# Fetching the first self-attention stacks in three places, reordering DVE's finish and maxima, and storing the last rows tile by tile

## The chip, the cores and the metric

The kernel runs on one core of one Trainium2 chip. The metric is the device time of one execution in microseconds. Engines are named as in the profile: PE multiplies matrices, DVE and ACT are the vector and the scalar engine, POOL is the general one, SP issues nearly all DMAs.

## What is computed

Two transformer layers over x of 8 batches of 512 rows and 512 columns, in float32. The first is a cross-attention on a context of 77 rows with adaptive layer norm. The second is a block with self-attention, cross-attention and an MLP. The parts that matter here, from the reference:

```
x_norm = modulate(_ln(x), shift_a, scale_a)
qkv = x_norm @ W_qkv + b_qkv
...
attn_w = softmax(einsum('bhqd,bhkd->bhqk', q, k) * scale)     # 16 heads of 32
attn_out = einsum('bhqk,bhkd->bhqd', attn_w, v) ... @ W_proj + b_proj
x = x + gate_a[:, None] * attn_out
...
h = gelu(modulate(_ln(x), shift_m, scale_m) @ W_mlp1 + b_mlp1) @ W_mlp2 + b_mlp2
x = x + gate_m[:, None] * h
```

## The kernel before

Six stages follow each other over all 8 batches: preparation, the first cross-attention, qkv, self-attention, the second cross-attention, the MLP. Each stage keeps its result in device memory for the next. A matrix product is made of three products of high and low parts, so 12 matmuls of 128x512 make one 128x512 block of a product over 512 rows. Work is split in tiles of 128 rows (NT = 4 of a batch) and in groups of four heads (G = 4 of a batch, 32 groups in all).

The order of every engine is written by hand: one program (`run` of each stage) is walked once per engine, and each step emits what that engine does for it, or nothing. `braid` takes one step of each of its generators in turn; such a turn is called a round here. `weave` and `next(following)` pull steps of the next stage into this one. An engine executes its list in order, so what stands behind a wait waits too.

**qkv** (class `Qkv`). For each batch b it makes eight products of queries and keys, m = 0 to 7, and four of values. PE writes a product into one of three banks, ACT adds the bias and writes the high part into one of three slots of `out_parts` (L1590), DVE the low part (L1531), SP stores both (L1512). ACT may overwrite a slot when its store has landed; PE may overwrite a bank when DVE has read it. Between the products the norm of batch b + 1 is made (`turning`): SP loads 1 MB into `norm_x` right behind the first store of the batch (L302), DVE takes statistics (L312) between the low parts of m = 3 and m = 4, normalises (L321) around that of m = 6, and PE turns the rows from the end of m = 7 on (L354). In the batches 6 and 7 the first maxima of self-attention are woven in.

**The first stacks.** Self-attention's group n needs a query stack and a key stack in local memory. `fetch(n)` issues six DMAs of 256 KB on SP (L1731, L1734), and on DVE, for n under 4, a fill of two rows with ones (L1801). In `SelfAttention.run`, fetch(0), fetch(1), fetch(2) and load_values(0) make up one step; `Qkv.run` pulls it at the end of batch 4. Whatever SP issues later, the next store and the load of `norm_x` too, is behind them.

**Self-attention** (class `SelfAttention`). A group n has 16 rounds. In each PE makes one block of scores (L1899), on which ACT takes an exponential (L1977), and one block of scores of group n + 2 (L1878), whose row maxima DVE takes (L1813, the maxima). There are two banks for scores, so PE's score i waits for exponential i - 2, and three for the maxima. `finish(n - 1)` closes the group before: ACT copies its heads out (L1990, round 2); DVE turns the sums (L1827, round 10), inverts them (L1830), spreads them (L1833), multiplies (L1839, round 13); ACT takes the high part of the result (L1999, between the exponentials of rounds 14 and 15), DVE the low part (L1844, round 15). POOL adds pairs of exponentials, 128x2048 in one operation (L1779), twice a group. PE's sums (L1933) and value products (L1921) come in bursts. `max_rows` turns the maxima of group n + 1 in round 2. In the second to fourth group of a batch PE has the projection of the batch before between the scores: from round 4 on in the second group, from round 0 in the third (six matmuls a round) and the fourth (three).

The braid of a group before:

```
yield from braid(s.attend(n), s.maxima(n + self.MAX) ..., after(2, s.max_rows(...)) ..., s.finish(n - 1) ..., *side)
```

**MLP** (class `Mlp`). Per batch 16 hidden blocks j. PE's down products of block j go into four accumulators, one per tile, three matmuls each (L2177); they trail the up products by two blocks. After the last up product (j = 15) come the down products of 13, 14 and 15. Then `residual`: DVE multiplies each accumulator by the gate (L2144), adds it to `x_rows` (L2146), and SP stores the batch, 1 MB, when all four are done (L2111).

## Time and profile before

| what | value |
|---|---|
| times of three runs | 2584.04, 2582.30, 2569.95 us; median 2582.3 |
| the profiled execution, its own time | 2574.66 us |
| its span | 2572.9 us |
| granted PE clock, mean | 0.972 of full |
| busy, share of the span | PE 93%, DVE 54%, ACT 40%, POOL 23% |
| DMA | 354 MB, 138 GB/s in the mean |

The span is what the rows below cut up; 1.8 us lie around it. The matmuls' ends are modelled, so PE's share says more of how densely they were issued than of spare time. The stages by time in the span: qkv from about 500 to 825 us, self-attention from 825 to 1475, the MLP from about 1856 to the end. Times of the rows count from the start of the span.

### The profile page before, as it was taken

To read this page: it belongs to the slowest core of one execution; us is meant where nothing else is said; L and a number is where in the kernel's file an instruction comes from. 1 tells how busy PE (TensorE), PEld (TensorE's weight loads), DVE (VectorE), ACT (ScalarE), POOL (GpSimd) and SP (SyncE) were. 2 spreads that over 40 slices of the span, in tenths; PEclk is the share of its full clock that TensorE was granted. 3 is DMA by queue.
4 is the path that set the end of the run, shared out by engine and by line. 5 is a ranking of instruction groups with operands and counts; after the bars stand their busy time and mean duration, and the time that the engine had idled before them with its cause. 6 is when DMAs were issued, how large, how long until landed. Compare 5 with 4: busy or idle time off the path is not lost. (4 is left out here: it accounts for less than half of the span.)

```text
span 2572.9 us, 32327 instructions
## 1 busy us (share of the span) xinstructions
PE 2401.8 (93%) x12048; PEld 1683.8 (65%) x12048; DVE 1380.0 (54%) x2463; ACT 1026.1 (40%) x1831; POOL 588.1 (23%) x325
## 2 busy tenths in 40 slices
PE   6889999999979899999998789999899999999998
PEld 5656666678867344444444456766588888888887
DVE  4566666644546877776777456676743222222221
ACT  3454444423322455555554334444442322233231
POOL 2101111110000466665665411111211011101100
PEclk9899999999989899999999899999999999999999
DMA  6687777554564446565453568786531101110110
GB/s 205 193 216 229 206 216 200 173 197 176 180 212 147 104 112 153 132 153 130 116 144 90 146 157 221 200 230 184 166 114 58 58 1 58 58 58 1 58 42 17
DMA packets 261275, 354.19 MB, mean 138 GB/s; under 512 B 60979, under 2 KB 109195, under 8 KB 261118
## 3 DMA queue, kind: packets, MB, share of 16 engines
q1 hardware_dynamic: 259950, 348.27, 47.9%
q0 software_dynamic: 1168, 3.85, 0.4%
q8 instruction: 96, 1.57, 0.3%
q14 instruction: 61, 0.50, 0.1%
HBM read 233.78 MB, written 116.69 MB: 136 GB/s over the span
## 5 line engine op out<-in xcount | busy, mean ns | idle before, releaser
L1813 DVE TENSOR_REDUCE negated_max<-banks 128x1 f32<-128x512 f32 x512 | 331.8, 675 | 140.7 <-PE banks L1878 140.4
L1977 ACT ACTIVATE self_exponentials<-banks 128x512 f32<-128x512 f32 x512 | 286.3, 594 | 283.8 <-PE banks L1899 133.0
L1779 POOL TENSOR_TENSOR self_exponentials<-self_exponentials,self_exponentials 128x2048 f32<-128x2048 f32 x64 | 303.1, 4736 | 217.0 <-ACT self_exponentials L1977 217.0
L2177 PE MATMUL banks<-mlp_w_down_hi,out_parts 128*128 128x512 f32 x1024 | 333.8, 389 | 0.1
L337 POOL TENSOR_SCALAR norm_rstd<-norm_mean_var 128x4 f32<-128x4 f32 x32 | 8.0, 249 | 1336.3 <-DVE norm_mean_var L316 1336.3
L2134 DVE TENSOR_TENSOR out_parts<-wide,out_parts 128x512 fp32r<-128x512 f32 x128 | 93.1, 727 | 371.6 <-ACT out_parts L2206 371.6
L1899 PE MATMUL banks<-self_query_stack,self_key_stack 98*128 98x512 f32 x512 | 236.4, 463 | 26.3 <-ACT self_exponentials L1977 23.5
L2196 ACT ACTIVATE wide<-banks,bias_columns 128x512 f32<-128x512 f32 x128 | 88.3, 690 | 426.0 <-PE banks L396 425.9
L1899 PEld LDWEIGHTS banks<-self_query_stack,self_key_stack 98*128 98x128 f32 x512 | 98.1, 192 | 212.6 <-ACT self_exponentials L1977 173.3
L2177 PEld LDWEIGHTS banks<-mlp_w_down_hi,out_parts 128*128 128x128 f32 x1024 | 192.2, 188 | 40.4 <-DVE cross_last_x_rows L1261 0.5
L1878 PE MATMUL banks<-self_key_stack,self_query_stack 96*128 96x512 f32 x512 | 207.4, 408 | 2.3 <-DVE negated_max L1813 2.1
L2177 PE MATMUL banks<-mlp_w_down_lo,out_parts 128*128 128x512 f32 x512 | 199.2, 389 | 0.0
L1217 DVE TENSOR_REDUCE negated_max<-banks 128x4 f32<-128x308 f32 x256 | 121.0, 473 | 100.4 <-PE banks L396 96.7
L1921 PE MATMUL banks<-self_exponentials,self_values 128*32 128x512 f32 x1024 | 140.4, 621 | 0.7 <-ACT self_exponentials L1977 0.7
L312 DVE BATCH_NORM_STATS2 norm_stats<-norm_x 128x6 f32<-128x512 f32 x128 | 84.6, 671 | 67.0 <-DMA norm_x<-x 66.7
L1400 ACT ACTIVATE cross_exponentials<-banks 77x512 f32<-77x512 f32 x128 | 75.3, 591 | 106.6 <-PE banks L1318 106.6
L377 ACT ACTIVATE wide<-banks,modulation_columns 128x512 f32<-128x512 f32 x96 | 74.5, 776 | 104.7 <-PE banks L354 97.3
L396 PE MATMUL banks<-x_hi,w_qkv_hi 128*128 128x512 f32 x256 | 101.2, 395 | 16.0 <-DVE out_parts L1531 15.1
L1590 ACT ACTIVATE out_parts<-banks,bias_columns 128x512 fp32r<-128x512 f32 x64 | 44.1, 689 | 179.6 <-PE banks L396 144.1
L1400 ACT ACTIVATE L_exponentials<-banks 77x512 f32<-77x512 f32 x128 | 75.3, 591 | 87.9 <-PE banks L1318 87.7
L2177 PEld LDWEIGHTS banks<-mlp_w_down_lo,out_parts 128*128 128x128 f32 x512 | 96.1, 188 | 20.0
L1878 PEld LDWEIGHTS banks<-self_key_stack,self_query_stack 96*128 96x128 f32 x512 | 99.8, 195 | 14.2 <-DVE negated_max L1813 5.6
(208 smaller groups left out, 5253.4 us busy)
## 6 DMA issues: line engine op xcount, KB each, us to landing
L_query_stack<-q_parts_L SPq DMA_DIRECT2D x96, 256.0 KB, 4.8
norm_x<-x SPq DMA_DIRECT2D x24, 1024.0 KB, 7.5
self_query_stack<-q_parts_self SPq DMA_DIRECT2D x96, 256.0 KB, 4.0
self_key_stack<-k_parts_self SPq DMA_DIRECT2D x96, 256.0 KB, 6.3
cross_query_stack<-q_parts_cross SPq DMA_DIRECT2D x96, 256.0 KB, 5.0
x_rows<-x SPq DMA_DIRECT2D x23, 1024.0 KB, 6.7
x<-x_rows SPq DMA_DIRECT2D x22, 1024.0 KB, 5.0
q_parts_L<-out_parts SPq DMA_DIRECT2D x32, 512.0 KB, 4.6
```

The source lines that it names most:

```text
L396: mm = e.matmul(out_ap, l, r, start=i == 0, stop=i == len(terms) - 1)
L1217: e.tensor_reduce(k.nm[n % 2][:, t:GH * NT:NT], k.bank[:, bk, 0:GH * S].rearrange("p (h k) -> p h k", k=S), AX_X, ALU.max, negate=True).th ...
L1400: e.activation(self.p[:, i % self.HEADS_KEPT, :], k.bank[0:S, self.scores.of["score", i], :], ACT.Exp, scale=SCALE).then_inc(self.exp.sem, 1)
L1779: e.tensor_tensor(self.p[kt - 1][:], self.p[kt - 1][:], self.p[kt][:], ALU.add).then_inc(self.paired.sem, 1)
L1813: e.tensor_reduce(k.nm[n % 2][:, h * NT + t:h * NT + t + 1], k.bank[:, self.max_banks.of["max", i], :], AX_X, ALU.max, negate=True).then_i ...
L1878: e.matmul(k.bank[:, bk, :], self.q[n % 4][0:ST, h, t * P:(t + 1) * P], self.keys[n % 4][0:ST, h, :], start=True, stop=True).then_inc(self ...
L1899: e.matmul(k.bank[:, bk, :], self.keys[n % 4][0:ST_MAX, h, kt * P:(kt + 1) * P], self.q[n % 4][0:ST_MAX, h, :], start=True, stop=True).the ...
L1921: mm = e.matmul(k.bank[h * HD:(h + 1) * HD, bk, :], self.v[n % 3][:, kt, h * HD:(h + 1) * HD], self.p[kt][:, h, :], start=kt == 0, stop=kt ...
L1977: e.activation(self.p[kt][:, h, :], k.bank[:, self.scores.of["score", i], :], ACT.Exp, scale=SCALE).then_inc(self.exp.sem, 1)
L2134: e.tensor_tensor(h[:, 1, :], k.wides[k.wide_turns.of["up", i]][:], raw(h[:, 0, :]), ALU.subtract).then_inc(self.lo.sem, 1)
L2177: mm = e.matmul(bank, l, w, start=j == 0 and q == 0, stop=j == JC - 1 and q == 2)
L2196: e.activation(k.wides[w][:], k.bank[:, self.banks.of["up", i], :], ACT.Gelu_apprx_tanh, bias=k.bias_cols[:, col:col + 1]).then_inc(self.w ...
```

## The change

1. `SelfAttention.run` now makes three steps of the first fetches: fetch(0); fetch(1); fetch(2) with load_values(0). `Qkv.run` pulls the first at the end of batch 4, the second in batch 5 after the product m = 4, the third at the end of batch 5.
2. In the braid of a self-attention group `finish(n - 1)` stands ahead of `maxima` and `max_rows`.
3. In the last batch of the MLP the down products of j = 14 and 15 run tile by tile, and the rows are stored in four DMAs of 256 KB, each behind its tile's addition.

```diff
@@ Qkv.run @@
                 if b >= B - 2:
                     weave(some(b - B + 3, following))
+                elif b == B - 3 and m == G:
+                    next(following)
                 yield
...
             weave(turning)
-            if b == B - 4:
+            if B - 5 < b < B - 2:
                 next(following)
@@ SelfAttention.run @@
         for n in range(self.FETCH):
             s.fetch(n)
-        s.load_values(0)
-        yield
+            if n == self.FETCH - 1:
+                s.load_values(0)
+            yield
...
-            yield from braid(s.attend(n), s.maxima(n + self.MAX) if n + self.MAX < LAST else None,
-                             after(2, s.max_rows(n + self.ROWS)) if n + self.ROWS < LAST else None,
-                             s.finish(n - 1) if n else None, *side)
+            yield from braid(s.attend(n), s.finish(n - 1) if n else None, s.maxima(n + self.MAX) if n + self.MAX < LAST else None,
+                             after(2, s.max_rows(n + self.ROWS)) if n + self.ROWS < LAST else None, *side)
@@ Mlp.run @@
-            for j in range(JC - self.LAG + 1, JC):
-                s.down(b, j)
+            rest = range(JC - self.LAG + 1, JC)
+            if b < B - 1:
+                for j in rest:
+                    s.down(b, j)
+            else:
+                for t in range(NT):
+                    for j in rest:
+                        s.down(b, j, (t,))
             s.residual(b)
@@ Mlp.sync @@
         def residual(b):
+            if b == B - 1:
+                for t in range(NT):
+                    sp.wait_ge(*self.added(b * NT + t))
+                    e.dma_start(k.out[b, t * P:(t + 1) * P, :], k.x[:, t, :]).then_inc(self.last_stored.sem, 16)
+                return
```

DVE's wait in `residual` follows the new count of down steps in the last batch (`last_step`), and the last batch's stores have a semaphore of their own.

SP from the last value stores of qkv's batch 4 on, before:

```order
L1517 DMA v_self<-qkv_value_rows_145 128x512
L1731 DMA self_query_stack_148<-q_parts_self 32x4x512 x3
L1734 DMA self_key_stack_152<-k_parts_self 32x4x512 x3
L1731 DMA self_query_stack_149<-q_parts_self 32x4x512 x3
L1734 DMA self_key_stack_153<-k_parts_self 32x4x512 x3
L1731 DMA self_query_stack_150<-q_parts_self 32x4x512 x3
L1734 DMA self_key_stack_154<-k_parts_self 32x4x512 x3
L1708 DMA self_values_162<-v_self 128x4x128
L1512 DMA q_parts_self<-out_parts_66 128x2x512
L302 DMA norm_x<-x 128x4x512
```

and with the change:

```order
L1519 DMA v_self<-qkv_value_rows_145 128x512
L1733 DMA self_query_stack_148<-q_parts_self 32x4x512 x3
L1736 DMA self_key_stack_152<-k_parts_self 32x4x512 x3
L1514 DMA q_parts_self<-out_parts_66 128x2x512
L302 DMA norm_x<-x 128x4x512
L1514 DMA q_parts_self<-out_parts_64 128x2x512
L1514 DMA q_parts_self<-out_parts_65 128x2x512
L1514 DMA q_parts_self<-out_parts_66 128x2x512
L1514 DMA k_parts_self<-out_parts_64 128x2x512
L1733 DMA self_query_stack_149<-q_parts_self 32x4x512 x3
L1736 DMA self_key_stack_153<-k_parts_self 32x4x512 x3
```

Six stack DMAs instead of eighteen stand ahead of batch 5's first store and its norm load. The third six, with the values, stand in the same way ahead of batch 6's first store and norm load. DVE's three fills move with them.

DVE in rounds 9 to 15 of a group, before:

```order
L1827 STREAM_TRANSPOSE sums_turned<-banks 128x512
L1813 TENSOR_REDUCE negated_max_83<-banks 128x1
L1830 RECIPROCAL reciprocals_turned<-sums_turned 128x16
L1813 TENSOR_REDUCE negated_max_83<-banks 128x1
L1833 STREAM_TRANSPOSE sums_turned<-reciprocals_turned 128x512
L1813 TENSOR_REDUCE negated_max_83<-banks 128x1
L1839 TENSOR_TENSOR heads_float_1_79<-heads_float_1_79,sums_turned 128x512
L1813 TENSOR_REDUCE negated_max_83<-banks 128x1 x2
L1844 TENSOR_TENSOR heads_parts_73<-heads_float_1_79,heads_parts_73 128x512
L1813 TENSOR_REDUCE negated_max_84<-banks 128x1 x3
```

and with the change, where one maximum fewer stands ahead of the first row:

```order
L1829 STREAM_TRANSPOSE sums_turned<-banks 128x512
L1815 TENSOR_REDUCE negated_max_83<-banks 128x1
L1832 RECIPROCAL reciprocals_turned<-sums_turned 128x16
L1815 TENSOR_REDUCE negated_max_83<-banks 128x1
L1835 STREAM_TRANSPOSE sums_turned<-reciprocals_turned 128x512
L1815 TENSOR_REDUCE negated_max_83<-banks 128x1
L1841 TENSOR_TENSOR heads_float_1_79<-heads_float_1_79,sums_turned 128x512
L1815 TENSOR_REDUCE negated_max_83<-banks 128x1 x2
L1846 TENSOR_TENSOR heads_parts_73<-heads_float_1_79,heads_parts_73 128x512
L1815 TENSOR_REDUCE negated_max_83<-banks 128x1
L1815 TENSOR_REDUCE negated_max_84<-banks 128x1 x3
```

The whole chain is one maximum further ahead, and the maximum of round 15 comes behind the low part. On ACT the copy of the heads (L1990) and the high part of the turned maxima (L1962) change places in round 2.

## Rows read from the trace of the kernel before

**Rows 1.** Timeline, ACT, qkv: start, duration, line, operation, [idle before, releaser].

```profile
665.02 0.69 ACT L1590 ACTIVATE out_parts<-banks,bias_columns 128x512 fp32r<-128x512 f32 x1 [4.06 <-PE banks L396]
...
699.62 0.69 ACT L1590 ACTIVATE out_parts<-banks,bias_columns 128x512 fp32r<-128x512 f32 x1 [4.06 <-PE banks L396]
...
752.38 0.69 ACT L1590 ACTIVATE out_parts<-banks,bias_columns 128x512 fp32r<-128x512 f32 x1 [4.06 <-PE banks L396]
```

**Rows 2.** Timeline, PE, the same stage.

```profile
683.86 0.60 PE L354 MATMUL banks<-identity,norm_x 128*128 128x128 f32 x4
...
728.59 0.80 PE L396 MATMUL banks<-x_hi,w_qkv_hi 128*128 128x512 f32 x1 [15.14 <-DVE out_parts L1531]
```

**Rows 3.** Timeline, SP (its DMA issues), same place.

```profile
698.04 1.65 SPq L1731 DMA_DIRECT2D self_query_stack<-q_parts_self  x3
```

**Rows 4.** Windows, PE and DMA: stretch, length, busy us by engine, granted clock, DMA share, GB/s.

```profile
698.00:721.00 23.00, 15.45 (x67) 12.14 (x66) 7.46 (x6) 2.07 (x3) 0.00 (x0) 0.91 1.01 219
721.00:727.00 6.00, 0.00 (x0) 0.00 (x0) 0.40 (x1) 0.69 (x1) 0.00 (x0) 0.50 1.07 376
```

**Rows 5.** Timeline, DVE, same place.

```profile
675.43 1.29 DVE L312 BATCH_NORM_STATS2 norm_stats<-norm_x 128x6 f32<-128x512 f32 x2 [3.49 <-DMA norm_x<-x]
...
682.73 0.99 DVE L321 TENSOR_SCALAR norm_x<-norm_x,norm_mean_var,norm_rstd 128x512 f32<-128x512 f32 x2
...
698.07 1.76 DVE L1801 MEMSET self_key_stack<- 2x2048 f32 x1 [0.48 <-issue]
...
726.60 1.28 DVE L312 BATCH_NORM_STATS2 norm_stats<-norm_x 128x6 f32<-128x512 f32 x2 [20.07 <-DMA norm_x<-x]
```

**Rows 6.** Waits, 832 to 1440 us: engine, line, releaser: us, times, longest.

```profile
ACT heads_parts L1999 <- DVE heads_float L1839: 23.7, 30, 1.6
PE banks L1899 <- ACT self_exponentials L1977: 23.5, 31, 1.9
```

**Rows 7.** Timeline, ACT and PE, a group's last rounds.

```profile
983.51 0.62 ACT L1999 CAST heads_parts<-heads_float 128x512 fp32r<-128x512 f32 x1 [0.73 <-DVE heads_float L1839]
...
984.68 0.50 PE L1899 MATMUL banks<-self_query_stack,self_key_stack 98*128 98x512 f32 x1 [1.04 <-ACT self_exponentials L1977]
```

**Rows 8.** Timeline, PE, into a group with projection work.

```profile
1041.35 0.50 PE L1899 MATMUL banks<-self_query_stack,self_key_stack 98*128 98x512 f32 x1 [0.34 <-ACT self_exponentials L1977]
```

**Rows 9.** Timeline, DVE, the same group as rows 7.

```profile
979.10 0.69 DVE L1813 TENSOR_REDUCE negated_max<-banks 128x1 f32<-128x512 f32 x1 [1.71 <-PE banks L1878]
979.71 0.70 DVE L1827 STREAM_TRANSPOSE sums_turned<-banks 128x512 f32<-128x512 f32 x1
...
984.60 0.68 DVE L1844 TENSOR_TENSOR heads_parts<-heads_float,heads_parts 128x512 fp32r<-128x512 f32 x1
```

**Rows 10.** Timeline, POOL's addition, DVE's slow subtraction, PE's wait.

```profile
984.71 4.99 POOL L1779 TENSOR_TENSOR self_exponentials<-self_exponentials,self_exponentials 128x2048 f32<-128x2048 f32 x1 [4.29 <-ACT self_exponentials L1977]
...
864.55 4.99 DVE L266 TENSOR_TENSOR self_w_p_lo<-weight_stage,self_w_p_hi 128x512 fp32r<-128x512 f32 x1
...
870.20 0.29 PE L1887 MATMUL banks<-identity,negated_max 128*16 128x128 f32 x1 [2.94 <-DVE negated_max L1813]
```

**Rows 11.** Timeline, the end, DVE, PE and SP.

```profile
2557.83 0.69 DVE L2134 TENSOR_TENSOR out_parts<-wide,out_parts 128x512 fp32r<-128x512 f32 x1 [4.75 <-ACT out_parts L2206]
...
2566.57 0.68 DVE L2144 TENSOR_TENSOR wide<-banks,mlp_gate_and_bias 128x512 f32<-128x512 f32 x1
...
2559.20 0.39 PE L2177 MATMUL banks<-mlp_w_down_lo,out_parts 128*128 128x512 f32 x1
...
2563.97 0.39 PE L2177 MATMUL banks<-mlp_w_down_lo,out_parts 128*128 128x512 f32 x1
...
2568.00 0.39 SPq L2111 DMA_DIRECT2D out<-x_rows  x1
```

**Rows 12.** Lines L2111 and L1517 of SP: issue to landing, us.

```profile
DMA to landing us min/median/max: 4.3/4.3/4.3
...
DMA to landing us min/median/max: 2.0/2.0/2.6
```

More of the change, by code:

```diff
@@ L2024, in __init__ @@
         c = k.count
-        self.x_loaded, self.x_stored = c("dma_x_rows", B, 16), c("dma_x_out", B, 16)
+        self.x_loaded, self.x_stored = c("dma_x_rows", B, 16), c("dma_x_out", B - 1, 16)
+        self.last_stored = c("dma_last_rows_out", NT, 16)
         self.gate_loaded = c("dma_mlp_gate", B, 32)
@@ L2058, in hidden_slot, with last_step @@
         return (2 * G * (B - 1) + i) % 3
+    def last_step(self, b, t):
+        return (b * JC + JC - 1) * NT + t if b < B - 1 else (b + 1) * JC * NT - 1 - (NT - 1 - t) * (self.LAG - 1)
     def set_freed(self, parts, x, gt, wides, third_out):
@@ L2138, in residual @@
                 i = b * NT + t
-                dve.wait_ge(*self.down((b * JC + JC - 1) * NT + t))
+                dve.wait_ge(*self.down(self.last_step(b, t)))
                 dve.wait_ge(*self.gate_loaded(b))
@@ L2161, in up, with down @@
                           self.norm.chunk(pe, b))).then_inc(self.up.sem, 1)
-        def down(b, j):
+        def down(b, j, tiles=range(NT)):
             i = b * JC + j
@@ L2168, in down @@
             pe.wait_ge(*self.w.ready(self.down_at[j]))
-            for t in range(NT):
+            for t in tiles:
                 if j == 0:
```

## Prediction

> **What bounds the kernel now.** I read the page first: PE is busy for 93% of the span, no other engine for more than 54%, so time is lost where PE stands still, and the change acts at three such places. I took each with the timeline of its stretch, then the waits by line.
>
> *In qkv* the first product of a batch is a ruler [rows 1]: batch 4 begins at 665.02, batch 5 at 699.62, batch 6 at 752.38. A batch takes 34.60 us, and batch 5 takes 52.76: **18.2 us too many**. The same turn shows on PE [rows 2]: in batch 4 it turns the normalised rows from 683.86 on, without a pause; in batch 5 it has waited 15.14 us at 728.59. SP is the reason: at 698.04 it issues the first of 18 stack fetches in a row [rows 3]. Each is 256 KB, 4.7 MB in all; at the 219 GB/s of the following 23 us [rows 4] they take 21.5 us, with every DMA engine busy. Behind them come the store and the 1 MB of `norm_x`, in a stretch at 376 GB/s in which PE does nothing and its granted clock is 0.50, the lower of its two levels, 1.2 GHz [rows 4]. DVE gets the rows at 726.60 after 20.07 us of waiting; in batch 4 it got them at 675.43 after 3.49 [rows 5].
>
> *In self-attention* the waits by line give ACT 23.7 us in 30 waits of the high part (L1999) for DVE's product (L1839), and PE 23.5 us in 31 waits of a score for an exponential [rows 6]. They are one chain: ACT takes the high part 0.73 us late, exponential 15 stands behind it, and PE's second score of the next group at 984.68 has waited 1.04 us [rows 7]. Into a fourth group, where projection matmuls lie between the scores, PE waits 0.34 [rows 8]; into a third, with six of them, I found no wait.
>
> *At the end* DVE and one last store stand behind PE's last matmul, and nothing runs beside them.
>
> **A, the fetches.** No DMA goes away. Ahead of batch 5's norm load stand six fetches instead of eighteen: 1.57 MB at 219 GB/s, 7.2 us; then the store, 512 KB, and 1 MB of rows: 1.57 MB again, at the 376 GB/s that such loads reached [rows 4] 4.2 us. Of the 28.56 us between 698.04 and 726.60 the before has 2.9 left when 21.5 and 4.2 are taken off; for the start of the burst I take 1.9 of these, since some is its drain. That is 13.3 us, near 711.3, or 11.7 us behind batch 5's first product. In batch 4 the rows came 10.4 us behind it (675.43 less 665.02), DVE's last normalised pair ended at 683.72 and PE took them at 683.86 [rows 2, 5]. So there is no slack, and what comes later than in batch 4 counts fully: 1.3 us. The fill of the second fetch (1.76 us, L1801) [rows 5] now lies in DVE's norm work in the middle of batch 5; less the part of a wait that it fills, 1.1. Batch 5 costs 2.4. The twelve DMAs' issuing and traffic in mid-batch have cover: the next norm load is a batch away, and each slot of `out_parts` is needed only two products after its store. Batch 6's boundary is as batch 5's, with 256 KB of values more (1.2 us at 219 GB/s) and DVE with maxima to take: 3. Gain 18.2 - 5.4 = **12.8 us**. Bounds: 18.2 if both late loads are absorbed, 6 if each boundary loses a third of what one lost.
>
> **B, the finish ahead of the maxima.** In rounds 9 to 15 DVE's list is the same but for one maximum, which comes last. At 979.10 DVE has waited 1.71 us for a block and only then turns the sums (0.70, L1827) [rows 9]. Now the turn fills that gap, and a maximum (0.69, some 0.6 in sequence) leaves the chain: the product is 1.2 to 1.3 us sooner. ACT's mean wait is 23.7 / 30 = 0.79, and 1.6 at the longest [rows 6]: nearly all of it goes, and next in line is PE's own rate. The gain is what PE felt. It has 16 places of the first kind [rows 7], 16 x 0.79 = 12.6, six of the second [rows 8], 6 x 0.34 = 2.0, and eight without. Sum **14.7 us** of the 23.5. Zero is the lower bound, if another wait follows; 18 the upper, with some of the other waits on exponentials. The maximum put last belongs to a group two ahead, with three banks behind it, and ACT's exchange in round 2 moves a copy past row maxima that are not needed before the next group: nothing. L1844 must begin before POOL's addition, which starts when exponential 15 ends: 984.60 against 984.71 [rows 9, 10], 0.11 us. That becomes about 0.5, since the product comes sooner by more than exponential 15 does.
>
> **C, the end.** PE takes 0.68 us for a tile's three matmuls: from 2559.20, block 14, to 2563.97, the last tile of block 15 [rows 11], seven such steps. Tile by tile, a tile is done every 1.36 us, and DVE's pair takes 1.33 (2 x 0.68). So DVE begins the last pair behind PE's last matmul, at 2564.65 instead of 2566.57: 1.9 us. Low part 15 is ready at 2558.52 (2557.83 and 0.69), and PE now wants it at 2559.88, 1.4 us later: hidden. The stores: SP issued 1 MB at 2568.00 and it landed 4.3 us later [rows 11, 12]; 256 KB of qkv's values land after 2.0 [rows 12]. That saves 2.3, and three earlier quarters go during DVE's pairs. **4.2 us.** Bounds: 1.9, if the landing does not shrink, and 4.9. Here a page speaks against the change. The row shows 2.0 us for one 256 KB transfer. The Trainium skill, "DMA: Bandwidth & Descriptors", section "Rules for kernel authors", wants 1 MiB per DMA for full bandwidth and small transfers put together. Should the four queue one behind another, see the fourth rival.
>
> The sum is 12.8 + 14.7 + 4.2 = **31.7 us**. From the profiled execution's 2574.66 that gives 2543; it was 7.6 us below the median of the three runs, 2582.3, and the mean of all four is 2577.7, which gives 2546. I say **2545**.
>
> **The rivals.** *One: the fetches still hold the norm.* The boundaries are now two, and the first burst's 7.2 us were costed at nearly nothing because other loads have their place behind it. If each costs 8 us or more (SP waits, the rate of 219 GB/s holding for the norm too, 7.2 us instead of 4.2, and PE's return at the low clock), A gives about 1, the sum is 20 and the time 2557. For it: no slack [rows 2]. Against: two thirds of the bytes have gone from the spot. *Two: B's time goes into the next wait.* ACT is one step from PE in every round, and DVE's maxima come later. Then only A and C count, 17: 2561. For it: ACT waits in many places; against: in rows 7 PE waits longer than ACT. *Three, the slower side: L1844 loses its place to POOL.* POOL's addition of 4.99 us begins at the end of exponential 15, and where DVE's subtraction (L266, the same form) met it, it took 4.99 us instead of 0.68, and PE waited 2.94 for a maximum [rows 10]. The chain now ends ACT's part sooner as well; if exponential 15 gained more than L1844 did, by over 0.5 us, the subtraction would fall into every addition: 30 groups x 2.94 = 88 lost, 17 gained, 2648. Against: both start from the same product, and L1844 has one step less before it. This stretch has a page, too: the Trainium skill, "GPSIMD Engine Reference", section 1, says POOL shares its interfaces to local memory with DVE, and names DVE instructions with two inputs there; the trace agrees, 4.99 against 0.68. *Four: small stores queue.* The first quarter is issued at 2559.20 + 1.36 + 1.33 = 2561.9. If they go one after another and each takes the 4.3 us of the only store to the output that a row shows [rows 12], the last lands at 2579.1 instead of 2572.3: C costs 6.8 instead of giving 4.2, and the time is 2556. Against: at 2.0 us each [rows 12] they would be through at 2569.9 even so. *Five: the order moves but no wait does* (DVE's gap [rows 9] is then the block's and not the turn's, and the rows load late for a reason other than the fetches): C alone, about 2573.
>
> **How the numbers follow.** Forecast 0.63; rivals one 0.13, two 0.12, three 0.03, four 0.04, five 0.05. The sum at its upper bounds is 41 us (18.2, 18, 4.9); A at its lower bound with B half met (7) and C at 1.9 makes 15: 2537 to 2563, and the runs shown lie up to 8 us from that mean. The range, 2531 to 2562, takes in rivals one, two and four. This kernel's measurement can tell 0.5%, 13 us, from no change: faster means below 2565. Forecast, rivals one, two and four lie there, with some 0.07 of them, where two terms fail together, on the wrong side: faster 0.85; same 0.10, slower 0.05.
>
> **What would show it.** Batch 5 of qkv takes 37 us and batch 6 no more than 3 over its old length; DVE's L312 waits about 5 us and not 20; PE has no idle of 15. ACT's wait for the product (L1839 before) falls from 23.7 to under 5 us, PE's for exponentials from 23.5 to about 9, and the subtraction of L1844 keeps its 0.68. The last store is issued near the end less 2.0 us, and the one before it 1.3 sooner. Wrong would be: an idle stretch of over 5 us at a batch boundary, PE's scores waiting for the same sum under another releaser, or subtractions of 2 to 5 us on DVE.

## The result and the profile after

| what | before | after |
|---|---|---|
| median | 2578.7 us (2569.95 to 2584.04, four runs) | 2551.9 us (2542.04 to 2553.79, four runs) |
| ratio, 95% interval | | 0.9888 [0.9856, 0.9921] |
| span of the profiled execution | 2572.9 | 2550.1 |
| busy, share of the span | PE 93%, DVE 54% | PE 94%, DVE 55% |

The change makes the kernel 1.1% faster, 29 us by the ratio. A second measurement on another chip, below, gives 0.9858. The forecast was 2545, with a range of 2531 to 2562. In the changed kernel the lines from qkv on stand two further down, those of the MLP's last stores and products 15 to 18.

The first products of the batches 5, 6 and 7 of qkv, timeline of ACT, after; [rows 1] has the same line before:

```profile
710.10 0.69 ACT L1592 ACTIVATE out_parts<-banks,bias_columns 128x512 fp32r<-128x512 f32 x1 [4.06 <-PE banks L396]
...
746.90 0.69 ACT L1592 ACTIVATE out_parts<-banks,bias_columns 128x512 fp32r<-128x512 f32 x1 [4.06 <-PE banks L396]
...
786.63 0.69 ACT L1592 ACTIVATE out_parts<-banks,bias_columns 128x512 fp32r<-128x512 f32 x1 [4.51 <-PE banks L396]
```

Batch 5 takes 36.80 us instead of 52.76. Batch 6 takes 39.73; before it took 37.44. Both together give 13.7 us. The norm of batch 6, timeline of DVE in batch 5, answers to [rows 5], and PE's first turn to [rows 2]:

```profile
721.47 1.29 DVE L312 BATCH_NORM_STATS2 norm_stats<-norm_x 128x6 f32<-128x512 f32 x2 [4.45 <-DMA norm_x<-x]
...
726.02 1.76 DVE L1803 MEMSET self_key_stack<- 2x2048 f32 x1 [0.48 <-issue]
...
730.05 0.99 DVE L321 TENSOR_SCALAR norm_x<-norm_x,norm_mean_var,norm_rstd 128x512 f32<-128x512 f32 x2
```

```profile
731.11 0.66 PE L354 MATMUL banks<-identity,norm_x 128*128 128x128 f32 x4 [1.93 <-DVE norm_x L321]
```

The rows reach DVE 11.37 us behind the batch's first product, and the forecast was 11.7; the 10.4 of batch 4 before [rows 1, 5] are missed by 1.0. Then the second stack's fill of 1.76 us stands in DVE's list, ahead of the normalising; DVE's last normalised pair begins 19.95 us behind the first product instead of 17.71, and PE waits 1.93 us. That is batch 5's 2.2 us.

Self-attention, waits by line (engine, line, releaser: us, times, longest), after, the stretch as long as in [rows 6]:

```profile
PE banks L1880 <- DVE negated_max L1815: 5.1, 3, 4.6
...
PE banks L1901 <- ACT self_exponentials L1979: 4.9, 18, 0.8
...
ACT heads_parts L2001 <- DVE heads_float L1841: 1.1, 2, 0.9
```

ACT's wait for the product is gone but for two, and PE's for exponentials goes from 23.5 to 4.9 us. A wait of 4.6 us for a maximum, at one place, is longer than what stood there before. The subtraction of [rows 9] has more room in front of POOL's addition, 0.46 us where it had 0.11, timelines of DVE and POOL:

```profile
973.21 0.68 DVE L1846 TENSOR_TENSOR heads_parts<-heads_float,heads_parts 128x512 fp32r<-128x512 f32 x1
```

```profile
973.67 4.65 POOL L1781 TENSOR_TENSOR self_exponentials<-self_exponentials,self_exponentials 128x2048 f32<-128x2048 f32 x1 [3.45 <-ACT self_exponentials L1979]
```

Once a batch it takes 1.80 us, beside POOL's additions for the projection (L1764); before it took 1.79 there, so the change has no part in that.

The end, timelines of DVE and SP and the landing of the last stores, answers to [rows 11, 12]:

```profile
2539.33 0.69 DVE L2152 TENSOR_TENSOR out_parts<-wide,out_parts 128x512 fp32r<-128x512 f32 x1 [4.75 <-ACT out_parts L2224]
...
2546.11 0.69 DVE L2162 TENSOR_TENSOR wide<-banks,mlp_gate_and_bias 128x512 f32<-128x512 f32 x1
```

```profile
2543.48 4.41 SPq L2126 DMA_DIRECT2D out<-x_rows  x4
```

```profile
DMA to landing us min/median/max: 2.0/2.0/2.0
```

The last pair begins 6.8 us behind the start of the last low part (8.7 before), and each of the four quarters lands 2.0 us after its issue. From the start of that low part to the end of the span it is 10.8 us, and it was 15.0.

These stretches say 13.7, 17.1 and 4.3 us, 35 in all, but the spans differ by 22.8. The gap lies ahead of the change, where both programs are the same: the first product of qkv comes at 509.47 before and 520.78 after. In the windows view of that stretch, before and after, the number behind the five engines' busy times is PE's granted clock:

```profile
150.00:450.00 300.00, 284.05 (x1710) 197.23 (x1709) 194.15 (x407) 142.42 (x261) 40.98 (x36) 0.97 0.79 217
```

```profile
150.00:450.00 300.00, 283.98 (x1665) 198.19 (x1664) 188.74 (x397) 139.26 (x255) 37.99 (x34) 0.94 0.78 213
```

0.94 instead of 0.97 over 300 us of the first cross-attention. Of the twelve kernels below ten began qkv between 507.5 and 512 us; two began at 516.0 and 519.2, with 0.96 and 0.94 there. An execution differs by some 10 us for this, whatever the kernel. So below a part is read from its own stretch, and the timed ratio is its check.

### The profile page after: what moved, and what is told of

Read it like the earlier page. It is cut to its first block, busy times and chain, and to the rows that moved or that the text cites. A ratio compares the mean times of both kernels' runs of the same rounds, so it can differ in the third digit from the quotient of the medians.

```text
span 2550.1 us, 32330 instructions
## 1 busy us (share of the span) xinstructions
PE 2408.3 (94%) x12048; PEld 1688.5 (66%) x12048; DVE 1390.8 (55%) x2463; ACT 1025.2 (40%) x1831; POOL 582.4 (23%) x325
## 4 chain that ended last, share of the span: by engine, by line
PE 81%; DVE 7%; ACT 4%; issue 3%; DMA 3%; SPq 1%; POOL 1%; DVEq 0%; ACTq 0%; POOLq 0%
PE banks L396 43%; PE banks L2195 14%; PE banks L1901 6%; PE banks L1923 4%; PE banks L1880 4%; PE banks L1935 2%; PE banks L1318 2%; PE banks L1332 2%; PE banks L1339 2%; PE banks L354 2%; DMA norm_x<-x 1%; ACT wide L377 1%; DVE negated_max L1815 1%; DVE norm_x L321 1%; PE banks L765 1%
## 5 line engine op out<-in xcount | busy, mean ns | idle before, releaser
L1781 POOL TENSOR_TENSOR self_exponentials<-self_exponentials,self_exponentials 128x2048 f32<-128x2048 f32 x64 | 294.5, 4602 | 202.5 <-ACT self_exponentials L1979 202.5
L329 DVE TENSOR_TENSOR x_lo<-wide,x_hi 128x512 fp32r<-128x512 f32 x80 | 56.3, 704 | 94.0 <-ACT x_hi L379 93.8
```

What stands on the lines that cost most here:

```text
L1781: e.tensor_tensor(self.p[kt - 1][:], self.p[kt - 1][:], self.p[kt][:], ALU.add).then_inc(self.paired.sem, 1)
```

## The experiments

The table has all of them. Batch 5 and 6 are the distances of their first products in qkv. *Stage* reaches from ACT's last product of queries and keys in qkv to its last high part of heads in self-attention; *first three* and *last batch* are the distances between the high parts of groups 0 and 3, and of groups 27 and 31. *End* reaches from the start of the MLP's last low part to the end of the span. All us, from one profiled execution each; the median and the ratio are of timed runs against the kernel before on the same chip. The rounds in these names count from 1, those of the text on the kernel before from 0: round 8 is `after(7, ...)`. (The expectation of the first try counts from 0.)

| kernel | median | ratio, 95% | batch 5 | batch 6 | stage | first three | last batch | end |
|---|---|---|---|---|---|---|---|---|
| before | 2578.7 | | 52.8 | 37.4 | 664.2 | 62.8 | 100.1 | 15.0 |
| the change | 2551.9 | 0.9888 [0.9856, 0.9921] | 36.8 | 39.7 | 647.1 | 56.7 | 101.5 | 10.8 |
| fetches alone | 2564.0 | 0.9951 [0.9927, 0.9975] | 37.5 | 39.5 | 664.0 | 59.9 | 102.3 | 15.0 |
| order alone | 2561.5 | 0.9935 [0.9910, 0.9959] | 53.1 | 37.4 | 649.9 | 56.3 | 102.3 | 15.0 |
| end alone | 2572.6 | 0.9969 [0.9952, 0.9987] | 53.2 | 37.4 | 663.5 | 59.9 | 101.6 | 10.8 |
| order alone, ACT's kept | 2560.2 | 0.9913 [0.9882, 0.9944] | 53.1 | 37.4 | 646.6 | 56.3 | 101.6 | 15.0 |
| the change again | 2541.6 | 0.9858 [0.9831, 0.9885] | 38.0 | 40.2 | 648.4 | 57.6 | 101.9 | 10.8 |
| + splits in round 8 | 2556.3 | 0.9916 [0.9882, 0.9949] | 37.1 | 39.8 | 653.6 | 57.5 | 102.8 | 10.8 |
| + fetches in mid-batch | 2541.0 | 0.9858 [0.9828, 0.9889] | 34.6 | 37.6 | 647.8 | 57.5 | 100.8 | 10.8 |
| + all three, first try | 2555.6 | 0.9904 [0.9877, 0.9931] | 34.6 | 37.7 | 656.9 | 59.6 | 101.0 | 10.8 |
| + splits in round 6 | 2534.0 | 0.9815 [0.9784, 0.9846] | 36.7 | 39.9 | 636.1 | 48.8 | 101.4 | 10.8 |
| + norm in round 7 | 2544.8 | 0.9860 [0.9826, 0.9895] | 37.4 | 40.2 | 650.1 | 57.5 | 101.3 | 10.8 |
| + all three, norm in round 7 | 2526.2 | 0.9791 [0.9756, 0.9826] | 34.6 | 38.4 | 636.8 | 49.1 | 102.3 | 10.8 |
| + all three, norm in round 6 | 2516.3 | 0.9760 [0.9738, 0.9781] | 34.6 | 38.0 | 627.1 | 48.7 | 94.3 | 10.8 |

**Each part by itself.** Before, with the three hunks on fetches and nothing else:

> The three fetch steps alone, on the kernel before. Theory one (each boundary waits for its own burst only): the first products of the last batches of qkv are 36.8 us apart (batch 5) and 39.7 (batch 6) instead of 52.8 and 37.4, so 13.7 us are gained there; DVE gets norm_x about 13 us behind the burst in batch 5; self-attention keeps its waits (ACT for the product 23.7 us in 30, PE for exponentials 23.5) and its length, the first batch included. Time 13 to 14 us under the kernel before. Rival (part of what self-attention gained in the pair, 6 us in its first batch against 1.7 in each later one, comes from the fetches, since stacks and clock are in another state when it begins): the first batch of self-attention is 4 us shorter here too, and the time 18 us lower.

Measured: batches 5 and 6 take 77.1 us instead of 90.2, 13.1 gained, and the stage of self-attention is as long as before, 664.0. ACT still waits 22.4 us for the product. The ratio gives 12.6 us. Theory one holds in time. The rival falls by the stage, though one thing surprised: the first three steps took 59.9 us here and not 62.8.

Before, with the one line of the braid:

```diff
-            yield from braid(s.attend(n), s.maxima(n + self.MAX) ..., after(2, s.max_rows(n + self.ROWS)) ..., s.finish(n - 1) ..., *side)
+            yield from braid(s.attend(n), s.finish(n - 1) ..., s.maxima(n + self.MAX) ..., after(2, s.max_rows(n + self.ROWS)) ..., *side)
```

> The new order of a group alone. Theory one: ACT's wait for DVE's product goes from 23.7 to under 1 us and PE's for exponentials from 23.5 to about 5; later batches are 1.6 to 1.9 us shorter, the first one 6, since PE's two waits in a row (1 us for an exponential, 2.9 for a maximum behind the weight's low part that POOL's addition holds up) are what brings its clock down there, and with the first gone the slow stretch is shorter (granted clock 0.92 instead of 0.85 in its second and third group); 17 us in all, qkv unchanged at 52.8 for batch 5. Rival (the first batch's extra comes from the fetches): the first batch gains 2 us as the others do, 13 us in all.

Measured: the stage takes 649.9 us, 14.3 less, and qkv is unchanged. ACT's wait, waits view:

```profile
ACT heads_parts L1998 <- DVE heads_float L1838: 2.0, 4, 0.9
```

The later batches take 73.2 to 73.8 instead of 75.0. The first three steps are 56.3. Set against 62.8 that would be 6.5, but the two kernels with the old order that were profiled since, fetches alone and end alone, took 59.9. Against these two stand six profiles of the new order with the splits in their old place, 56.3 to 57.6: **the order is worth some 3 us there, and the other 3 were in the one profile of before**. Theory one was wrong in that number, and its rival's reason, the fetches, was wrong too.

Before, with the tile by tile end:

> The tile by tile end alone. Theory: from the last low part of the hidden blocks to the end of the span 10.8 us instead of 15.1; the last pair on DVE begins 1.9 us sooner, each quarter lands 2.0 us after its issue. Time 4.3 us under the kernel before, which the timed rounds can't tell from none. Rival (quarters queue): the last lands 4 us or more after its issue and the end is 13 us or more behind the low part.

Measured: the end takes 10.8 us, 4.3 less. The ratio gives 8 us with an interval from 3 to 12, so the timing agrees with the 4.3 and sees it better than I expected. The quarters do not queue: the change's own four landed 2.0 us after their issue.

**ACT's exchange.** The new order for DVE, the old one for ACT:

```diff
-            yield from braid(s.attend(n), s.finish(n - 1) ..., s.maxima(n + self.MAX) ..., after(2, s.max_rows(n + self.ROWS)) ..., *side)
+            yield from braid(s.attend(n), after(2, s.max_rows(n + self.ROWS)) ..., s.finish(n - 1) ..., s.maxima(n + self.MAX) ..., *side)
```

> The new order of a group with ACT's copy of the heads left behind the row maxima as before (finish goes between max_rows and maxima in the braid). Theory one (ACT's exchange is worth nothing, DVE's order is all): self-attention as in the kernel with the whole new order, within 1 us over the stage. Rival (the earlier copy of the heads frees PE's bank or shortens ACT's list at a group's start): 0.2 to 0.3 us a group are lost again, 6 to 10 us in all, seen as ACT's or PE's wait in rounds 2 to 4.

Measured: a stage of 646.6 us, at least as short as with the exchange (647.1 to 649.9). The exchange is worth nothing, as costed.

**The change again.**

> The whole change once more, on the chip and beside the runs of the kernels that build on it. Theory (the parts add up: fetches 13, finish 16, end 4): 33 us under the kernel before, 0.987 of it; qkv's batches 5 and 6 at 36.8 and 39.7 us, self-attention's later batches at 73.2, its first three group steps 56.4, the end 10.8. Rival (the parts take from each other): under 25 us, with one of these stretches longer than in the kernels that have its part alone.

Measured: 0.9858, 36.7 us by the ratio. The parts alone make 12.6 + 16.8 + 8.0 = 37 by their ratios, and 13.1 + 16.0 + 4.3 = 33 by their stretches (16.0 is the mean of the three stages with the old order, 663.9, less the mean, 647.9, of the five new ones: the change twice, the order alone twice, mid-batch fetches). Its own stretches make 12.1 + 15.8 + 4.3 = 32. They add up. Batches 5 and 6 are 1.0 us longer here than with the fetches alone (78.1 and 77.1), which is half of the rival's sign; its other half, a total under 25 us, did not come, and it falls.

**Where the first batch of self-attention loses its time.** In both orders its first two steps take about 20 us and more, the third 16 to 17. Windows from high part to high part, groups 0 to 3, columns as in [rows 4]; first the old order (end alone), then the new one (ACT's order kept):

```profile
866.72:888.23 21.51, 17.37 (x82) 6.61 (x81) 17.49 (x24) 10.66 (x21) 9.55 (x2) 0.92 0.42 99
888.23:909.49 21.26, 18.74 (x82) 6.83 (x81) 17.57 (x24) 10.66 (x20) 9.55 (x2) 0.84 0.36 88
909.49:926.60 17.11, 15.64 (x82) 6.29 (x81) 12.66 (x23) 10.01 (x20) 12.69 (x5) 1.00 0.73 201
```

```profile
863.74:883.80 20.06, 17.07 (x82) 6.81 (x81) 17.13 (x24) 10.55 (x22) 9.18 (x2) 0.91 0.44 106
883.80:903.88 20.08, 17.07 (x82) 6.54 (x81) 17.02 (x24) 10.53 (x21) 9.18 (x2) 0.92 0.42 93
903.88:920.07 16.19, 15.75 (x82) 6.30 (x81) 12.65 (x23) 9.82 (x21) 11.36 (x4) 1.00 0.82 212
```

The granted clock is 0.84 to 0.92 in the first two steps and 1.00 in the third. In the new order PE waits 2.69 and 2.71 us for a maximum in the first two; in the old one it waits 1.04 and 2.94 in the first, 1.03 and 1.33 in the second. In the third it waits for nothing over 1.04 in either. The long waits are those of [rows 10]: the low part of the projection's weights (L266) beside POOL's addition. First I put the split in the middle of the group:

```diff
-            if n < G:
-                s.split(self.wp_at + n)
...
-            side = []
+            side = [after(7, splits(n))] if n < G else []
```

> The changed kernel with the four splits of the projection's weights in self-attention's first batch (ACT's high part, DVE's low part) moved from a group's start to its round 8, when POOL does no addition. Theory one (the low part is held up by POOL's addition, 4.4 us instead of 0.7, PE waits 2.5 us for a maximum behind it, and its clock falls after that wait): low parts take 0.68, PE's four waits of 2.5 us go, the granted clock of the first batch is 1.00 and the group steps there are 16.3 us as the fourth is, 49 instead of 56.4 for three, 10 us in all with the first group. Rival one (the clock there has another reason): the waits go but the steps only fall to 18, 5 us in all. Rival two (another operation takes the place beside POOL's addition): no gain.

Measured: 2556 us, 15 more than the change on the same chip. The profiled executions differ by 9 us only: the stage is 5 us longer, 2 lie between it and the MLP, and 3 in the MLP, where nothing was touched. What makes those 5, and the rest of the timed difference, stays open. Timelines of POOL, DVE and PE:

```profile
840.10 4.55 POOL L1782 TENSOR_TENSOR self_exponentials<-self_exponentials,self_exponentials 128x2048 f32<-128x2048 f32 x1 [3.56 <-ACT self_exponentials L1980]
```

```profile
840.63 4.57 DVE L266 TENSOR_TENSOR self_w_p_lo<-weight_stage,self_w_p_hi 128x512 fp32r<-128x512 f32 x1 [0.17 <-ACT self_w_p_hi L260]
```

```profile
845.86 0.50 PE L1881 MATMUL banks<-self_key_stack,self_query_stack 96*128 96x512 f32 x1 [2.31 <-DVE negated_max L1816]
```

Rival two: in round 8 DVE's subtraction begins 0.5 us behind POOL's *other* addition of the group and takes 4.57 again. POOL's addition ends at 844.65 and the subtraction at 845.20, 0.55 later, with 0.69 of work of its own. Group 0, whose split had been free (there is no addition at its start), now pays as well: its high part comes 54.0 us after qkv's last product instead of 49.6. Two rounds sooner lies the gap between the additions (`after(5, splits(n))`):

> The split of the projection's weights in round 6 of its group instead of round 8: the kernel with round 8 met POOL's other addition (its low part began 0.5 us behind it and took 4.6 us again), while round 6 lies between the two. Theory (it is the meeting with the addition alone that costs): low parts 0.7 us, none of PE's waits of 2.3 to 3.2 us for a maximum, the first three group steps 49 instead of 57.5, 10 us under the changed kernel. Rival (PE's granted clock in that batch is low for another reason): the waits go and the steps stay at 53 or more, 5 us.

Measured: 0.9815, and a stage of 636.1 us, 12 under the change's 648. The additions of POOL, the subtraction between them, and the first two windows:

```profile
834.37 4.58 POOL L1782 TENSOR_TENSOR self_exponentials<-self_exponentials,self_exponentials 128x2048 f32<-128x2048 f32 x1 [2.08 <-ACT self_exponentials L1980]
842.56 4.58 POOL L1782 TENSOR_TENSOR self_exponentials<-self_exponentials,self_exponentials 128x2048 f32<-128x2048 f32 x1 [3.61 <-ACT self_exponentials L1980]
```

```profile
840.94 0.69 DVE L266 TENSOR_TENSOR self_w_p_lo<-weight_stage,self_w_p_hi 128x512 fp32r<-128x512 f32 x1 [0.17 <-ACT self_w_p_hi L260]
```

```profile
849.42:865.63 16.21, 15.64 (x82) 6.31 (x81) 13.44 (x24) 10.31 (x22) 9.21 (x2) 1.00 0.57 131
865.63:881.83 16.20, 15.63 (x82) 6.28 (x81) 13.43 (x24) 10.32 (x22) 9.21 (x2) 1.00 0.63 132
```

The subtraction takes 0.69, PE's long waits for a maximum in this batch are gone (one of 1.8 is left, in group 0), the clock is 1.00 and a step takes 16.2. The theory was right within 1 us: 48.8 for three steps. The clock's share can be read from a chance find. In the order alone a step with the same wait, 2.6 us, was granted 1.00; windows of that step:

```profile
882.90:901.55 18.65, 15.69 (x82) 6.19 (x81) 16.92 (x24) 10.64 (x21) 9.16 (x2) 1.00 0.43 100
```

It took 18.65 us. Without the wait a step takes 16.2, with it and at 0.92 20.1, at 0.84 21.1. So the wait costs 2.4 us, and the lower clock in its step 1.5 or 2.5 more. Why that one step kept its clock, no run shows.

**The fetches in mid-batch.**

```diff
-                elif b == B - 3 and m == G:
+                elif B - 5 < b < B - 2 and m == G:
                     next(following)
...
-            if B - 5 < b < B - 2:
-                next(following)
...
-        for n in range(self.FETCH):
+        for n in range(self.FETCH - 1):
             s.fetch(n)
-            if n == self.FETCH - 1:
-                s.load_values(0)
             yield
-        yield from s.maxima(0)
+        first = s.maxima(0)
+        yield from some(G, first)
+        s.fetch(self.FETCH - 1)
+        s.load_values(0)
+        yield from first
```

> The changed kernel with no fetch at a batch's boundary: fetch(0) in batch 4 after the product m = 4, fetch(1) there in batch 5, fetch(2) and the values in the middle of batch 6. Theory one (1.3 us of batch 5's 2.2 us too many are the six fetches ahead of the norm load, the rest the fill; batch 6 the same): batch 5 takes 35.5 us instead of 36.8 and batch 6 38 instead of 39.7, batch 4 takes 0.9 more than 34.6 for its fill; 2 us gained. Rival (the fill alone delays): batches 4 and 5 at 36.8 both, nothing gained.

Measured: batch 5 at 34.61 us, batch 6 at 37.58, batch 4 at 34.59: all but 0.1 of the loss is gone. Timelines of DVE and ACT:

```profile
706.67 1.28 DVE L312 BATCH_NORM_STATS2 norm_stats<-norm_x 128x6 f32<-128x512 f32 x2 [1.65 <-DMA norm_x<-x]
...
711.23 1.76 DVE L1803 MEMSET self_key_stack<- 2x2048 f32 x1 [0.48 <-issue]
```

```profile
698.11 0.69 ACT L1590 ACTIVATE out_parts<-banks,bias_columns 128x512 fp32r<-128x512 f32 x1 [4.06 <-PE banks L396]
...
732.72 0.69 ACT L1590 ACTIVATE out_parts<-banks,bias_columns 128x512 fp32r<-128x512 f32 x1 [4.06 <-PE banks L396]
...
770.30 0.69 ACT L1590 ACTIVATE out_parts<-banks,bias_columns 128x512 fp32r<-128x512 f32 x1 [4.51 <-PE banks L396]
```

Both theories fall in part. The rows now come 8.6 us behind the first product and DVE waits 1.65 us, and the same fill at the same place costs nothing. When it does cost, three batches 4 of other kernels show. In the end alone and in the first try the rows came nearly equally late, 11.0 and 10.8 us behind the first product, the first without a fill in mid-batch, the second with one; timelines of DVE:

```profile
677.82 1.29 DVE L312 BATCH_NORM_STATS2 norm_stats<-norm_x 128x6 f32<-128x512 f32 x2 [4.07 <-DMA norm_x<-x]
```

```profile
674.20 1.29 DVE L312 BATCH_NORM_STATS2 norm_stats<-norm_x 128x6 f32<-128x512 f32 x2 [3.91 <-DMA norm_x<-x]
...
678.75 1.76 DVE L1804 MEMSET self_key_stack<- 2x2048 f32 x1 [0.48 <-issue]
```

Batch 4 took 35.06 us in the first and 36.24 in the second; in the kernel with the norm in round 7 the rows came after 10.7 without a fill, and it took 34.73. So up to some 10.5 us the rows may come at no loss, each us behind that costs a whole one, and the fill, once they are that late, costs 1.35 more; if they come by 8.8 it costs nothing. For batch 5 of the change (11.4) that makes 0.85 + 1.35 = 2.2, what was measured. The stretches are 5.9 us shorter than in the change on that chip (72.2 instead of 78.1), which the ratio, 0.9858 both times, does not show: the interval is ±0.3%, 8 us. In the kernels with all three moves batch 6 took 38.4 and 38.0, so not every execution gets these 5.9.

**The norm beside POOL's addition.** The wait of 4.6 us in the waits of the change lies in the last batch. Timelines of DVE, POOL and PE, after:

```profile
1358.92 4.77 DVE L321 TENSOR_SCALAR norm_x<-norm_x,norm_mean_var,norm_rstd 128x512 f32<-128x512 f32 x1
...
1364.21 0.53 DVE L321 TENSOR_SCALAR norm_x<-norm_x,norm_mean_var,norm_rstd 128x512 f32<-128x512 f32 x1
```

```profile
1358.90 4.50 POOL L1781 TENSOR_TENSOR self_exponentials<-self_exponentials,self_exponentials 128x2048 f32<-128x2048 f32 x1
```

```profile
1364.34 0.79 PE L1880 MATMUL banks<-self_key_stack,self_query_stack 96*128 96x512 f32 x1 [4.63 <-DVE negated_max L1815]
```

The same place before:

```profile
1384.79 0.50 PE L1878 MATMUL banks<-self_key_stack,self_query_stack 96*128 96x512 f32 x1 [1.82 <-DVE negated_max L1813]
```

There L321 began 1.1 us behind the addition and took 4.15; the two later profiles of the old order have a wait of 3.45.

Normalising (L321) took 4.77 us at the start of POOL's addition and 0.53 at 1364.21. It has one tensor as input, where L266 has two. The Trainium skill, "SBUF — State Buffer", section "SBUF: two separate sides", says the shared pair of ports is locked by whichever of the two engines starts first, for a whole instruction, and counts instructions of DVE with two inputs in local memory and those in a mode that uses both ports. The traces agree for two inputs, with 4.57 against 0.69. That L321 runs in such a mode no row says; its 4.77 against 0.53 would fit. The first try moved this too, with the splits in round 8 and the fetches in mid-batch, but it moved the wrong steps:

```diff
-                side.append(some((1, 5, 4, 12, 12)[n - LAST], following))
+                side.append(after(6 if n == LAST - G else 0, some((1, 5, 4, 12, 12)[n - LAST], following)))
```

> Both of these moves, and the six steps of the next stage's norm that the fourth last group takes begin in its round 6, behind POOL's addition. Theory (the moves add, and PE's wait of 4.6 us at the last batch's first group goes, which the normalising beside POOL's addition made): 10 + 2 + 4, 16 us under the changed kernel, 0.981 of the kernel before. Rival (the steps moved later delay the next stage's first products by as much): 12 us under the changed kernel, and the last batch of self-attention keeps its 101.5 us.

Measured: 0.9904, slower than the change, and a stage 8.5 us longer; the splits in round 8 made 5 of that above, and 2 more lie in the step between the first two high parts, 22.8 us at a granted clock of 0.80. The fourth last group, with five steps of the norm, holds its statistics, the third last the normalising, and L321 still took 4.77 us. With `n == LAST - 3` instead, on the change alone:

> The changed kernel with the next stage's four normalising steps in the third last group begun in its round 7 instead of its round 1. Theory (beside POOL's addition the first took 4.8 us instead of 0.5, and PE waited 4.6 for a maximum behind it): L321 takes 0.5 each time, the wait is gone, self-attention's last batch takes 97 to 98 us instead of 101.5 to 102. Rival (the next stage's first products then wait for the norm): last batch unchanged, PE waits 4 us more for x_lo behind it.

Measured: no gain, 0.9860 against 0.9858, the last batch at 101.3. PE waits 3.65 us for a maximum in that group instead of 4.6, and the step between the high parts around it is 2.0 us shorter; but in the next step it waits 3.0 us for the norm's low part (L329) instead of 1.9, as the rival had it, and 1.6 us go again. In the kernel with all three moves it is the same:

> All three: fetches in mid-batch, splits in round 6, the norm's steps late. Theory (they add: 5 us in qkv by the stretches of the kernel with fetches in mid-batch, 34.6 and 37.6, then 10, then 4): 19 us under the changed kernel, 0.979 of the kernel before. Rival (one of the three takes another's gain): 12 us or less.

Measured: 0.9791, 17 us under the change by the two ratios. The stage is 11.6 shorter and qkv's two batches 5, which is the splits and the fetches; the norm gave nothing. Timelines of DVE, POOL and PE:

```profile
1342.42 4.17 DVE L321 TENSOR_SCALAR norm_x<-norm_x,norm_mean_var,norm_rstd 128x512 f32<-128x512 f32 x1
```

```profile
1341.59 4.72 POOL L1782 TENSOR_TENSOR self_exponentials<-self_exponentials,self_exponentials 128x2048 f32<-128x2048 f32 x1
```

```profile
1347.84 0.79 PE L1881 MATMUL banks<-self_key_stack,self_query_stack 96*128 96x512 f32 x1 [3.64 <-DVE negated_max L1816]
```

The first three take 0.5 to 0.9 us, the fourth begins 0.8 behind the next addition and takes 4.17. One round sooner none meets an addition for long:

> All three moves again, with the norm's four steps begun one round sooner (begun in round 7 the first three took 0.5 to 0.9 us, the fourth, at 1342.42, met POOL's next addition of 1341.59 and took 4.2). Theory (between two additions there is room for all four): no L321 over 1 us in that group, PE's wait of 3.6 us for a maximum gone, self-attention's last batch 98 us; 4 us under the kernel before it, 23 under the changed kernel. Rival (the wait returns as a later wait for x_lo, since the next stage's norm is on that path): the last batch 101 us and no gain over the kernel with round 7.

```profile
1334.61 1.22 DVE L321 TENSOR_SCALAR norm_x<-norm_x,norm_mean_var,norm_rstd 128x512 f32<-128x512 f32 x1
...
1339.89 0.90 DVE L321 TENSOR_SCALAR norm_x<-norm_x,norm_mean_var,norm_rstd 128x512 f32<-128x512 f32 x1
```

```profile
1330.94 4.59 POOL L1782 TENSOR_TENSOR self_exponentials<-self_exponentials,self_exponentials 128x2048 f32<-128x2048 f32 x1
...
1340.48 4.77 POOL L1782 TENSOR_TENSOR self_exponentials<-self_exponentials,self_exponentials 128x2048 f32<-128x2048 f32 x1
```

Measured: 0.9760, a last batch of 94.3 us instead of 102.3, and a median 9.9 us under the kernel with round 7. The first and the last of the four take 1.22 and 0.90 us: the first begins 0.9 us before the addition of 1330.94 ends, the last 0.6 before that of 1340.48 begins. PE has no long wait in that group. I expected 4 us and the stretch gave 8: again more than PE's wait of 3.6. Windows between the same two high parts, with round 7 and with round 6; the number behind the five engines is the granted clock:

```profile
1328.06:1351.76 23.70, 19.99 (x93) 9.47 (x93) 20.89 (x29) 9.92 (x21) 14.76 (x6) 0.88 0.08 24
```

```profile
1326.96:1345.83 18.87, 18.72 (x95) 9.09 (x95) 18.02 (x28) 10.03 (x21) 14.82 (x6) 1.00 0.10 30
```

4.8 of the 8 us lie in that step, whose clock is 1.00 instead of 0.88, and 2.6 in the next, where the wait for the norm's low part is 2.1 again. This version, 2516.3 us, beats both kernels: 2.4% under before, and 1% under the change by the two ratios.

## Why the prediction was right

The likeliest case came in, and each term can be set beside its stretch.

- **A, forecast 12.8 us.** The pair gives 13.7 and the fetches alone 13.1. Batch 5 was costed at 2.4 too many and has 2.2; over six kernels with three fetch steps at these places it has 2.1 to 3.4. Batch 6 was costed at 3 and has 2.1 to 2.8. The landing of the rows, 11.7 us behind the first product, was 11.4. That the cut of 18 DMAs to 6 frees the norm load was the step that carried it, and it held. The 2.4 were 1.3 for late rows and 1.1 for the fill, and the runs make it 0.85 and 1.35. That there is no slack was read from one batch, and this was luck: its rows came after 10.4 us, just at the limit of 10.5, while those of batch 3 came after 9.1. What the text had not seen is that the loss left over could go entirely: once the rows are early, neither is a term.
- **B, forecast 14.7 us.** Measured 16.0 over the stage, 14.0 to 17.3 by kernel. The later batches give 1.8 each; the forecast was 2 x 0.79 + 0.34 = 1.92. PE's wait for exponentials fell to 4.9 us and not to about 9. The third groups lose 0.2 each, where I had zero. The first batch gives 2.3 to 3.6 by kernel, and 0.7 more ahead of its first high part in the pair, where three places of 0.79 had made 2.4; the kernel with the least has clocks of 0.84 and 0.91 in its first two steps, the order alone 0.84 and 1.00. The clock was left out of the sum, and that it makes the difference is argued from these rows. The last batch, in which some 0.8 of the sum lay, gives nothing: 101.5 us with the change, 101.6 and 102.3 in the old order's later profiles. So part of the nearness is luck: the last batch was counted too high and the first too low, and the 17.1 of the pair hold about 3 that were in the one profile of before.
- **C, forecast 4.2 us.** Measured 4.3, as 1.9 from DVE's last pair and 2.3 from the landing, each as costed. The low part of block 15 was in time.
- **The rivals.** *The fetches still hold the norm*: no, 11.4 us behind the first product. *The next wait takes B's gain*: no. *L1844 loses to POOL's addition*: never to one of exponentials in these kernels, it kept its place by at least 0.46 us in the change, and 0.5 was said; but the mechanism is real, and it struck L266 and L321. *Small stores queue*: no; what counts at the end is the landing of the last store, 2.0 against 4.3 us. The rule of the Trainium skill that the prediction cites there, "DMA: Bandwidth & Descriptors", section "Rules for kernel authors", is one for bandwidth, and these four stores of 256 KB did not need it. *No wait moves*: no.
- **The number.** 33 us by the stretches of the parts against 31.7; 29 and 36.7 us by the two ratios. The median of 2551.9 lies 7 above the forecast, in the range; the 10 us by which an execution varies in the first cross-attention, with the change or without it, are more than the error of the sum.

## What to carry to other kernels

When one queue serves two purposes, ask for each long burst what waits behind it, and measure its lateness against the slack of a batch that is undisturbed: a burst in the middle of a batch was free here, the same at its start was not. A wait of an engine is worth what the engine at the bound feels behind it, 16 us of 23.7 here, and such a chain was shortened by changing two neighbours in a list. An instruction of DVE that met a long one on POOL took six to nine times its time here; look for the same line with two durations, and move it by one or two rounds rather than halfway, since the next meeting may be as near.

## What the runs showed of the hardware

- The same subtraction of 128x512 took 0.69 us between POOL's additions and 4.4 to 5.0 beside one, and in the row above ended 0.55 us after it. Normalising took 0.53 and up to 4.77. The maxima, which read from the matmuls' banks, took 0.68 in either place.
- PE's granted clock, 1.00 in self-attention's second to seventh batch, was 0.80 to 0.92 in nearly every step of its first batch that held a wait of 2.3 to 2.9 us (and in the old order in one with 1.0 and 1.3), and 1.00 in all when those waits were gone. In the last batch, too, the gain, 8 us, was about twice the wait.
- The same program before qkv took between 507.5 and 520.8 us, and the two longest had a granted clock of 0.94 instead of 0.97 in 300 us of the first cross-attention, the third one 0.96. What sets it off was not found.
- A store of 256 KB of the last rows landed 2.0 us after its issue, the one of 1 MB after 4.3.
